# Graph attention on one core: a batch's finishing kept in its PSUM bank, the key matrix placed ahead of a batch's last set, and one unit of work given from GpSimd to ScalarE

## The chip, the cores and the metric

The kernel runs on one core of a Trainium2 chip. The metric is the time of one execution on the device in microseconds (us); several executions were timed and the median is given. The engines are called PE (TensorE, matrix products), DVE (VectorE), ACT (ScalarE), POOL (GpSimd) and SP (SyncE, which issues the DMAs here).

## The reference

The input is x, 8 batches of 1024 rows with 64 channels, and one 1024 x 1024 adjacency matrix per batch. Four graph layers follow one another, each as `x = layernorm(x + layer(x, adj))`. The change concerns the first two, which compute an additive score through a hidden layer of 64 channels for every pair of rows:

```
# layer 0
h   = relu(fa[:, :, None, :] + fb[:, None, :, :])      # fa, fb = feat @ W1 parts
att = softmax(einsum('bijo,o->bij', h, W2) + mask)
out = einsum('bij,bjc->bic', att, feat)
# layer 1
lr     = leaky(vu[:, :, None, :] + iv[:, None, :, :])
scores = where(adj > 0, einsum('bijc,c->bij', lr, yita), -1e12)
agg    = leaky(softmax(scores) @ x)
out    = leaky((agg + (1 + beta) * x) @ linW.T + linb)
```

Layer 2 is a plain graph attention and layer 3 an attention with 8 heads and edge biases. The change doesn't touch them.

## The kernel before, in words

`additive_layers` computes the first two layers. There are 16 "batches" in a row, g = 0 to 15: eight of layer 0 (g < nb, nb = 8) and eight of layer 1. Each has 8 tiles j of 128 query rows, so there are K = 128 tiles k. For a tile the scores of 128 rows against 1024 keys are built in one PSUM tensor, `psS`. The hidden values of 4 rows and 32 channels make a unit, a 128 x 1024 fp32 tensor. PE multiplies units by a selection matrix and adds them up in `psS`. The units of a tile stand in 11 sets (s = 0 to 10) of four, one for each group q of 32 rows.

Units are made in three ways (`unit_sets`):

- A "merged" unit covers 64 channels at once. POOL clamps the keys `BLOS` into a slot of the ring `hid_p` (`clamp_unit`), and DVE takes a maximum of the upper keys, adds POOL's half and writes the slot in place (`merge_units`, one scalar_tensor_tensor). There are 20 in a tile.
- A "pool" unit is a half (32 channels) that POOL makes alone. The tuple POOL_ALONE lists them: 2 in a tile.
- "high" and "low" units are halves that ACT makes as a Relu with a bias (`hidden_units`) into the ring `hid_a`: 22 in a tile.

So POOL makes 22 units in a tile, DVE 20 and ACT 22. Both rings have 11 slots; a slot is free again when PE has used its set (`hid_used`). The upper keys of DVE come from PSUM (`psB`, put there by PE in `place_keys` at the start of a batch), except in sets 0 and 1 of a batch's first tile, where DVE reads a copy in SBUF, `BHI`.

One tile later the softmax of a tile follows: DVE subtracts the mask and takes the minimum (`masked_min`, after its units of set 0), ACT takes the exponential (`exponentials`, set 1), PE transposes (`turn`, set 3), ACT and DVE each copy one half to SBUF (`copy_low`, `copy_high`, set 5), and PE weighs the rows (`weigh`, a tile later).

When the 8 tiles of a batch are through, the batch g - 1 is finished during the tiles of g. The steps stand at fixed places (tile j, set s) in each engine's order, `aux_jobs` for PE and ACT and `batch_steps` for DVE: PE's `fold` writes the bank `psA` in tile 2, DVE's `scale` divides it by the softmax sums at (2, 7) and writes `y` in SBUF, and then `add_rows` (residual, bn_stats, bn_aggr) and `normalise` (subtract the mean, multiply by the deviation) work on `y`. Layer 1 has leaky_relu, a query product and a linear map between them. POOL computes the deviation in `inverse_deviation`, and in tile 3 the bounds of the next batch (`bounds`). In the same tiles the next batch is projected: PE transposes its rows (`turn_x`, also in `psA`) and makes queries, low keys and high keys, one job in tile 0's set 3 and one at the end of each of the tiles 0, 1 and 2. ACT copies each result to SBUF; the last three at its set 0 of the next tile.

The order of every engine is written out by hand; there is no planner.

Of the kernel before, what the change touches and what calls it, by code (L numbers as in the profile page):

```python
# [12 lines left out]
P = 128  # L13
# [10 lines left out]
POOL_ALONE = ((1, 3), (3, 7))  # L24
# [25 lines left out]
def additive_layers(nc, adj, X, rest, later, w, buf, small, ident, nb, n):  # L50
# [64 lines left out]
    with ExitStack() as ctx:  # L115
# [90 lines left out]
        def _(pe):  # L206
            def aux(k, job):
# [7 lines left out]
                if what == "turn_x":  # L215
                    if layer:
                        pe.wait_ge(x_written, g - nb + 1)
                    elif g == 1:
                        pe.wait_ge(rest_loaded, 16)
                    pe.nop(nofuse=True)  # L220
# [98 lines left out]
            for job in projection(0):  # L319
                aux(0, job)  # L320
            for k in range(K + tiles):
                g, j = divmod(k, tiles)
                if k < K and j == 0:
                    place_keys(g)
# [4 lines left out]
                for s in range(SETS):  # L329
                    if k < K:  # L330
                        hidden_set(k, s)
                    if s == 3:
                        if 1 <= k < K + 1:
                            turn(k - 1)
                        for job in aux_jobs(k, 0):
                            aux(k, job)
# [4 lines left out]
        def _(act):  # L341
# [32 lines left out]

            def exponentials(k):
# [21 lines left out]
            for k in range(K + tiles):  # L397
                for s in range(SETS):
# [11 lines left out]
                    if s == 6:  # L410
                        for job in aux_jobs(k, 0):
                            aux(job)

        @block.vector
        def _(dve):
            def merge_units(k, s):
                g, j = divmod(k, tiles)
                if j == 0 and s == 0:
                    dve.wait_ge(aux_out, done("keys_high", g))
                    dve.wait_ge(bounds_ready, 4 * (g + 1))  # L420
                if j == 0 and s == 2:
                    dve.wait_ge(keys_placed, g + 1)
                for i, at_set, q, p in MERGED_UNITS:
                    if at_set == s:
                        at, m = k * NP + i, quad(j, q, p)
                        keys = BHI[:, g % 2, :] if j == 0 and s < 2 else psB[:, :]
                        dve.wait_ge(pool_made, at + 1)
                        dve.scalar_tensor_tensor(out=hid_p[:, at % RING_P, :], in0=keys, scalar=THI[:, g % 2, m:m + 1],  # L428
# [17 lines left out]
            def scale(g):  # L446
# [4 lines left out]
                dve.tensor_tensor(per_tile(y), per_tile(psA[:, :]), spread(rden), ALU.mult).then_inc(aux_out, 1)  # L451

            def add_rows(g):
# [4 lines left out]
                dve.tensor_tensor(y, y, rows(g), ALU.add).then_inc(y_ready, 1)  # L458
                dve.wait_ge(y_ready, g + 1)
                for t in range(tiles):  # L460
                    last = dve.bn_stats(stats[:, t, :], y[:, t * C:(t + 1) * C])
# [7 lines left out]
            def leaky_rows(g):  # L469
                dve.wait_ge(aux_out, done("fold", g))  # L470
                dve.scalar_tensor_tensor(out=y, in0=y, scalar=GAT_SLOPE, in1=y, op0=ALU.mult,
                                         op1=ALU.max).then_inc(leaky, 1)
                dve.wait_ge(leaky, g - nb + 1)
                dve.scalar_tensor_tensor(out=y, in0=rows(g), scalar=w["beta1"], in1=y, op0=ALU.mult,
                                         op1=ALU.add).then_inc(u_ready, 1)

            def linear_out(g):
                dve.wait_ge(aux_made, done("linear", g))
                dve.tensor_tensor(y.rearrange("p (h t c) -> p h t c", h=2, c=C),
# [3 lines left out]
                dve.wait_ge(aux_out, done("linear", g))  # L483
                dve.scalar_tensor_tensor(out=y, in0=y, scalar=GAT_SLOPE, in1=y, op0=ALU.mult,
                                         op1=ALU.max).then_inc(lin_leaky, 1)

            def normalise(g):
                dve.wait_ge(rstd_ready, g + 1)
                dve.tensor_tensor(per_tile(y), per_tile(y), mv[:, :, 0:1].to_broadcast([P, tiles, C]),
# [3 lines left out]
                dve.tensor_tensor(per_tile(out), per_tile(y), spread(rstd), ALU.mult).then_inc(x_written, 1)  # L493

            def batch_steps(g, j, s):
                if (j, s) == (2, 7):
                    scale(g)
                if g < nb:
                    if (j, s) == (2, 9):
                        add_rows(g)  # L500
                    if (j, s) == (4, 8):
                        normalise(g)
                else:
                    if (j, s) == (2, 9):
                        leaky_rows(g)
                    if (j, s) == (4, 2):
                        linear_out(g)
                    if (j, s) == (4, 9):
                        add_rows(g)
                    if (j, s) == (6, 8):  # L510
                        normalise(g)
# [939 lines left out]
```

## Time and profile before

| what | value |
|---|---|
| median of 3 runs | 5577.21 us (5561.33 to 5579.57) |
| the profiled execution's own time | 5561.66 us |
| its span, first to last instruction | 5559.8 us |
| mean granted TensorE clock | 0.942 |
| busy share of the span: PE, DVE, ACT, POOL | 84%, 93%, 84%, 74% |
| stage of the first two layers | 20 us to about 3828 us |

The busy share of an engine is the time in which it had an instruction, over the span. It is an average over stages with different limits. Durations of neighbouring instructions on one engine overlap a little, so what one costs in a row is read from the distance between two starts (called the pitch below).

### The profile page before, as it was taken

The page shows a single profiled execution, that of the slowest core. Times are in us where ns is not written, and L with a number is a line of the kernel's source. Part 1 is how long each engine was busy: PE and PEld are TensorE (multiplying, and loading weights), DVE is VectorE, ACT ScalarE, POOL GpSimd, SP SyncE. Part 2 cuts the span into 40 slices and gives each one's busy share as a digit, 9 for nine tenths or more (in the row PEclk, how much of TensorE's full clock was granted, in tenths as well). Part 3 has the DMA queues.
Part 4 walks back from the last instruction along what each step waited for, and adds up shares of the span by engine and source line. Part 5 has one row for each costly group of instructions (what it writes and reads, how often), then busy time and mean ns, then how long its engine had stood idle before and what let it go on. Part 6 is the DMA issues. An engine that isn't in the chain of part 4 may idle for free. (4 is left out here: it accounts for less than half of the span.)

```text
span 5559.8 us, 118931 instructions
## 1 busy us (share of the span) xinstructions
PE 4678.2 (84%) x48920; PEld 1837.8 (33%) x48920; DVE 5196.5 (93%) x5731; ACT 4667.0 (84%) x5649; POOL 4098.1 (74%) x3706
## 2 busy tenths in 40 slices
PE   7878788787887888888887888887789999999998
PEld 2222222222222222222222222223445554545444
DVE  7999999999999999999999999996769999999998
ACT  7889888898888888888887888886768888888887
POOL 8999999999999999999999999994312322222223
PEclk9999999999999999999999999998879999999999
DMA  1000000000000000000000000003510111011100
GB/s 41 20 20 20 16 20 20 20 20 16 20 20 20 17 20 20 16 20 20 16 20 20 16 20 19 18 16 96 156 34 27 34 34 34 26 34 34 37 26 15
DMA packets 144928, 155.32 MB, mean 28 GB/s; under 512 B 52294, under 2 KB 119622, under 8 KB 144390
## 3 DMA queue, kind: packets, MB, share of 16 engines
q1 hardware_dynamic: 143686, 147.65, 8.9%
q8 instruction: 391, 6.41, 0.5%
q14 instruction: 147, 1.20, 0.1%
q10 hardware_dynamic: 704, 0.07, 0.0%
HBM read 137.20 MB, written 2.10 MB: 25 GB/s over the span
## 5 line engine op out<-in xcount | busy, mean ns | idle before, releaser
L189 POOL TENSOR_SCALAR a_hid_p<-a_BLOS,a_PHI,a_PLO 128x1024 f32<-128x1024 f32 x2816 | 3356.8, 1206 | 164.0 <-PE apsS L315 150.7
L428 DVE SCALAR_TENSOR_TENSOR a_hid_p<-apsB,a_THI,a_hid_p 128x1024 f32<-128x1024 f32 x2496 | 3006.6, 1275 | 40.0 <-POOL a_hid_p L189 39.6
L315 PE MATMUL apsS<-a_hid_p,a_sel_high 128*32 128x512 f32 x11264 | 2680.7, 610 | 151.6 <-DVE a_hid_p L428 58.8
L315 PE MATMUL apsS<-a_hid_a,a_sel_high 128*32 128x512 f32 x6144 | 1927.3, 608 | 187.7 <-DVE a_hid_p L428 179.7
L315 PE MATMUL apsS<-a_hid_a,a_sel_low 128*32 128x512 f32 x5120 | 1718.1, 613 | 289.3 <-DVE a_hid_p L428 266.0
L353 ACT ACTIVATE a_hid_a<-a_BHI,a_ALH 128x1024 f32<-128x1024 f32 x1536 | 1679.7, 1143 | 0.0
L353 ACT ACTIVATE a_hid_a<-a_BLO,a_ALH 128x1024 f32<-128x1024 f32 x1280 | 1423.3, 1143 | 0.0
L315 PEld LDWEIGHTS apsS<-a_hid_p,a_sel_high 128*32 128x32 f32 x11264 | 613.7, 111 | 918.6 <-issue 545.2
L746 PE MATMUL m3S<-xT,Q 64*128 64x512 f32 x2048 | 601.7, 662 | 133.1 <-ACT x_even L790 90.2
L315 PEld LDWEIGHTS apsS<-a_hid_a,a_sel_low 128*32 128x32 f32 x5120 | 371.5, 111 | 864.1 <-DVE a_hid_p L428 578.1
L315 PEld LDWEIGHTS apsS<-a_hid_a,a_sel_high 128*32 128x32 f32 x6144 | 423.8, 110 | 704.4 <-DVE a_hid_p L428 383.2
L762 PE MATMUL m3O<-ZT,Xr 32*64 32x256 f32 x16384 | 576.7, 413 | 4.3 <-DVE ZT L839 4.3
L790 ACT ACTIVATE x_even<-m3S,bias 128x512 f32<-128x512 f32 x684 | 435.1, 690 | 142.0 <-PE m3S L746 120.5
L676 POOL TENSOR_TENSOR part<-prod 128x256 f32<-128x256 f32 x64 | 46.9, 732 | 581.9 <-DVE prod L865 581.9
L839 DVE STREAM_TRANSPOSE ZT<-x_even 128x1024 f32<-128x1024 f32 x342 | 421.8, 1236 | 54.0 <-ACT x_even L799 49.9
L762 PEld LDWEIGHTS m3O<-ZT,Xr 32*64 32x64 f32 x16384 | 358.0, 142 | 319.4 <-issue 222.0
L830 DVE CUSTOM_DVE_ANT_0 x_even<-x_even,mask 128x1024 f32<-128x1024 f32 x342 | 439.8, 1320 | 6.3 <-ACT x_even L790 5.9
L380 ACT ACTIVATE a_Z<-a_Z,small 128x1024 f32<-128x1024 f32 x128 | 146.9, 1148 | 316.4 <-DVE small L437 316.4
L799 ACT ACTIVATE x_even<-x_even,low 128x1024 f32<-128x1024 f32 x342 | 394.7, 1154 | 0.0
L689 POOL TENSOR_SCALAR vare<-mv 128x1 f32<-128x1 f32 x64 | 12.2, 190 | 394.7 <-DVE mv L878 394.7
L746 PEld LDWEIGHTS m3S<-xT,Q 64*128 64x128 f32 x2048 | 162.9, 190 | 335.9 <-ACT x_even L790 175.4
L790 ACT ACTIVATE Z<-m3S,bias 128x512 f32<-128x512 f32 x340 | 216.2, 690 | 61.8 <-PE m3S L746 50.8
(185 smaller groups left out, 4526.5 us busy)
## 6 DMA issues: line engine op xcount, KB each, us to landing
a_adj_in<-adj SPq DMA_DIRECT2D x128, 512.0 KB, 3.4
adj_in<-adj SPq DMA_DIRECT2D x128, 512.0 KB, 3.7
Xr<-x_odd SPq DMA_DIRECT2D x128, 64.0 KB, 2.1
out<-yn SPq DMA_DIRECT2D x64, 32.0 KB, 1.5
x_even<-x SPq DMA_DIRECT2D x1, 256.0 KB, 2.8
wqT<-L_wqT SPq DMA_DIRECT2D x1, 130.0 KB, 4.2
wkT<-L_wkT SPq DMA_DIRECT2D x1, 130.0 KB, 4.3
wvT<-L_wvT SPq DMA_DIRECT2D x1, 130.0 KB, 4.4
```

Source lines behind the costliest of these rows:

```text
L189: gp.tensor_scalar(hid_p[:, at % RING_P, :], BLOS[:, g % 2, :], PHI[:, g % 2, m:m + 1], PLO[:, g % 2, m:m + 1], ALU.min, ALU.max).then_inc ...
L315: last = pe.matmul(psS[32 * q:32 * q + 32, h * HALF:(h + 1) * HALF], sel[:, 28 - 4 * p:60 - 4 * p], unit, start=s == 0 and layer == 0, sto ...
L353: act.activation(hid_a[:, at % RING_A, :], keys[:, g % 2, :], ACT.Relu, bias=ALH[:, g % 2, int(kind == "high"), m:m + 1]).then_inc(act_mad ...
L380: act.activation(Z, Z, ACT.Exp, bias=lowest(k), scale=-1.0, accum_out=den[:, g % 2, j:j + 1]).then_inc(probs_ready, 1)
L428: dve.scalar_tensor_tensor(out=hid_p[:, at % RING_P, :], in0=keys, scalar=THI[:, g % 2, m:m + 1], in1=hid_p[:, at % RING_P, :], op0=ALU.ma ...
L676: gp.tensor_tensor(part[:, 0:4 * C], prod[:, 0:4 * C], prod[:, 4 * C:8 * C], ALU.add).then_inc(halved, 1)
L746: last = pe.matmul(psS[(at + e) % 3][:, :], Q[rows, t % 2, h, :], xT[rows, b % 2, half * HALF:(half + 1) * HALF], start=True, stop=True)
L762: last = pe.matmul(psO[C * e:C * e + C, a, 0:32 * HEADS], Xr[rows, b % 2, at * C:(at + 1) * C], ZT[rows, m % 3, at, :], start=step == 0, s ...
L790: act.activation(Z(k, e)[:, half * HALF:(half + 1) * HALF], psS[(4 * k + 2 * half + e) % 3][:, :], ACT.Prelu, bias=bias[:, b % 2, head:hea ...
L799: act.activation(Z(k, e), Z(k, e), ACT.Exp, bias=low[:, k % 4, e:e + 1], scale=-1.0, accum_out=den[:, m % 8, 2 * h + e:2 * h + e + 1]).the ...
L830: dve.tensor_tensor_reduce(out=Z(k, e), in0=Z(k, e), in1=mask[:, m % 2, :], scale=1.0, scalar=-LOWEST, op0=ALU.add, op1=ALU.min, accum_out ...
L839: dve.transpose(ZT[:, m % 3, :, at:at + 32], Z(k, e).rearrange("p (b i) -> p b i", i=32)).then_inc(turned, 1)
```

## The change

1. DVE no longer writes the batch's rows to `y` in SBUF after each step: `scale`, `add_rows`, `linear_out` and `normalise` read and write the PSUM bank `psA` in place. `y` keeps only the query rows of layer 1.
2. The two leaky_relu steps of layer 1 go from DVE (scalar_tensor_tensor on `y`) to ACT (Prelu in place in `psA`), at (2, 9) and (4, 5).
3. `normalise` moves from (4, 8) in layer 0 and (6, 8) in layer 1 to (7, 10) in both; `add_rows` of layer 1 moves from (4, 9) to (4, 8). The first PE job of a later batch waits for the `normalise` that used `psA` last.
4. PE runs `place_keys` of the next batch ahead of the last set of the current one, where it used to run at the start of the batch. DVE reads `psB` for all its units, and waits for the placed keys at a batch's first unit.
5. The unit (q, s) = (1, 3) leaves POOL_ALONE: a tile now has 21 POOL units, 20 DVE units and 23 ACT units.

```diff
-POOL_ALONE = ((1, 3), (3, 7))
+POOL_ALONE = ((3, 7),)
...
                 if what == "turn_x":
-                    if layer:
-                        pe.wait_ge(x_written, g - nb + 1)
-                    elif g == 1:
+                    if g == 1:
                         pe.wait_ge(rest_loaded, 16)
+                    if g >= 3:
+                        pe.wait_ge(x_written, g - 2)
...
+            place_keys(0)
             for k in range(K + tiles):
                 g, j = divmod(k, tiles)
-                if k < K and j == 0:
-                    place_keys(g)
...
                 for s in range(SETS):
+                    if s == SETS - 1 and j == tiles - 1 and g + 1 < G:
+                        place_keys(g + 1)
...
+            def leaky_rows(g):
+                act.wait_ge(aux_out, done("fold", g))
+                act.activation(psA[:, :], psA[:, :], ACT.Prelu, alpha=GAT_SLOPE).then_inc(leaky, 1)
+
+            def leaky_linear(g):
+                act.wait_ge(aux_out, done("linear", g))
+                act.activation(psA[:, :], psA[:, :], ACT.Prelu, alpha=GAT_SLOPE).then_inc(lin_leaky, 1)
...
+                    if g - 1 >= nb and (j, s) == (2, 9):
+                        leaky_rows(g - 1)
+                    if g - 1 >= nb and (j, s) == (4, 5):
+                        leaky_linear(g - 1)
...
                 if j == 0 and s == 0:
-                    dve.wait_ge(aux_out, done("keys_high", g))
                     dve.wait_ge(bounds_ready, 4 * (g + 1))
-                if j == 0 and s == 2:
                     dve.wait_ge(keys_placed, g + 1)
...
-                        keys = BHI[:, g % 2, :] if j == 0 and s < 2 else psB[:, :]
-                        dve.scalar_tensor_tensor(out=hid_p[:, at % RING_P, :], in0=keys, scalar=THI[:, g % 2, m:m + 1],
+                        dve.scalar_tensor_tensor(out=hid_p[:, at % RING_P, :], in0=psB[:, :], scalar=THI[:, g % 2, m:m + 1],
...
-                dve.tensor_tensor(per_tile(y), per_tile(psA[:, :]), spread(rden), ALU.mult).then_inc(aux_out, 1)
+                dve.tensor_tensor(per_tile(psA[:, :]), per_tile(psA[:, :]), spread(rden), ALU.mult).then_inc(aux_out, 1)
...
-                dve.tensor_tensor(y, y, rows(g), ALU.add).then_inc(y_ready, 1)
+                dve.tensor_tensor(psA[:, :], psA[:, :], rows(g), ALU.add).then_inc(y_ready, 1)
...
-            def leaky_rows(g):
-                dve.wait_ge(aux_out, done("fold", g))
-                dve.scalar_tensor_tensor(out=y, in0=y, scalar=GAT_SLOPE, in1=y, op0=ALU.mult,
-                                         op1=ALU.max).then_inc(leaky, 1)
+            def query_rows(g):
                 dve.wait_ge(leaky, g - nb + 1)
-                dve.scalar_tensor_tensor(out=y, in0=rows(g), scalar=w["beta1"], in1=y, op0=ALU.mult,
+                dve.scalar_tensor_tensor(out=y, in0=rows(g), scalar=w["beta1"], in1=psA[:, :], op0=ALU.mult,
                                          op1=ALU.add).then_inc(u_ready, 1)
...
-                dve.tensor_tensor(per_tile(y), per_tile(y), mv[:, :, 0:1].to_broadcast([P, tiles, C]),
+                dve.tensor_tensor(per_tile(psA[:, :]), per_tile(psA[:, :]), mv[:, :, 0:1].to_broadcast([P, tiles, C]),
                                   ALU.subtract).then_inc(centred, 1)
...
-                dve.tensor_tensor(per_tile(out), per_tile(y), spread(rstd), ALU.mult).then_inc(x_written, 1)
+                dve.tensor_tensor(per_tile(out), per_tile(psA[:, :]), spread(rstd), ALU.mult).then_inc(x_written, 1)
...
                 if g < nb:
                     if (j, s) == (2, 9):
                         add_rows(g)
-                    if (j, s) == (4, 8):
-                        normalise(g)
                 else:
-                    if (j, s) == (2, 9):
-                        leaky_rows(g)
+                    if (j, s) == (3, 1):
+                        query_rows(g)
                     if (j, s) == (4, 2):
                         linear_out(g)
-                    if (j, s) == (4, 9):
+                    if (j, s) == (4, 8):
                         add_rows(g)
-                    if (j, s) == (6, 8):
-                        normalise(g)
+                if (j, s) == (7, 10):
+                    normalise(g)
```

## Rows read from the trace of the kernel before

**Rows 1.** The page: span and busy time of each engine.

```profile
span 5559.8 us, 118931 instructions
...
PE 4678.2 (84%) x48920; PEld 1837.8 (33%) x48920; DVE 5196.5 (93%) x5731; ACT 4667.0 (84%) x5649; POOL 4098.1 (74%) x3706
```

**Rows 2.** Busy time in a stretch, then clock, DMA share, GB/s: first two layers.

```profile
20.00:3802.00 3782.00, 3133.53 (x27208) 979.03 (x27204) 3657.89 (x3285) 3215.44 (x3297) 3592.58 (x3038) 0.95 0.06 19
```

**Rows 3.** The line of `masked_min` (L437): duration ns min/median/max, first and last start.

```profile
L437 DVE CUSTOM_DVE_ANT_0 a_Z<-apsS,a_mask x128: 1206/1217/1226, 59.5 to 3801.1; 128x1024 f32<-128x1024 f32 x128
```

**Rows 4.** The same view: DVE's merged units, `normalise`, `add_rows` and `scale`.

```profile
L428 DVE SCALAR_TENSOR_TENSOR a_hid_p<-apsB,a_THI,a_hid_p x2496: 1248/1276/1287, 34.7 to 3797.6; 128x1024 f32<-128x1024 f32 x192
L428 DVE SCALAR_TENSOR_TENSOR a_hid_p<-a_BHI,a_THI,a_hid_p x64: 1273/2050/5594, 26.0 to 3567.8; 128x1024 f32<-128x1024 f32 x64
...
L489 DVE TENSOR_TENSOR a_y<-a_y,a_mv x16: 693/7959/8877, 391.9 to 3826.2; 128x512 f32<-128x512 f32 x16
...
L458 DVE TENSOR_TENSOR a_y<-a_y,x_even x8: 7049/7066/7076, 331.8 to 1967.2; 128x512 f32<-128x512 f32 x8
...
L451 DVE TENSOR_TENSOR a_y<-apsA,a_rden x16: 691/691/692, 326.4 to 3813.1; 128x512 f32<-128x512 f32 x16
```

**Rows 5.** DVE in order of time: start us, us, line, op, count [idle before].

```profile
1266.76 7.07 DVE L458 TENSOR_TENSOR a_y<-a_y,x_even 128x512 f32<-128x512 f32 x1
...
1275.64 4.82 DVE L428 SCALAR_TENSOR_TENSOR a_hid_p<-apsB,a_THI,a_hid_p 128x1024 f32<-128x1024 f32 x4
...
1345.02 1.23 DVE L437 CUSTOM_DVE_ANT_0 a_Z<-apsS,a_mask 128x1024 f32<-128x1024 f32 x1 [0.80 <-PE apsS L315]
...
1357.50 13.19 DVE L428 SCALAR_TENSOR_TENSOR a_hid_p<-apsB,a_THI,a_hid_p 128x1024 f32<-128x1024 f32 x11
1370.61 1.22 DVE L437 CUSTOM_DVE_ANT_0 a_Z<-apsS,a_mask 128x1024 f32<-128x1024 f32 x1
```

**Rows 6.** POOL in order of time.

```profile
24.66 9.97 POOL L189 TENSOR_SCALAR a_hid_p<-a_BLOS,a_PHI,a_PLO 128x1024 f32<-128x1024 f32 x5
...
1220.42 25.82 POOL L189 TENSOR_SCALAR a_hid_p<-a_BLOS,a_PHI,a_PLO 128x1024 f32<-128x1024 f32 x22
...
1247.47 12.91 POOL L189 TENSOR_SCALAR a_hid_p<-a_BLOS,a_PHI,a_PLO 128x1024 f32<-128x1024 f32 x11
...
1284.27 0.20 POOL L162 TENSOR_SCALAR a_vare<-a_mv 128x8 f32<-128x8 f32 x1
1284.55 1.65 POOL L164 TENSOR_TENSOR a_rstd<-a_vare,small 128x8 f32<-128x8 f32 x1
...
1293.74 0.41 POOL L172 TENSOR_SCALAR a_THI<-a_ALH 128x256 f32<-128x256 f32 x1
...
1296.30 11.73 POOL L189 TENSOR_SCALAR a_hid_p<-a_BLOS,a_PHI,a_PLO 128x1024 f32<-128x1024 f32 x10
```

**Rows 7.** ACT in order of time.

```profile
1226.53 0.58 ACT L393 ACTIVATE a_OT<-apsO 128x512 f32<-128x512 f32 x1
1227.01 1.15 ACT L353 ACTIVATE a_hid_a<-a_BHI,a_ALH 128x1024 f32<-128x1024 f32 x1
1228.05 1.15 ACT L353 ACTIVATE a_hid_a<-a_BLO,a_ALH 128x1024 f32<-128x1024 f32 x1
...
1245.36 1.03 ACT L366 ACTIVATE a_BLO<-apsT 128x1024 f32<-128x1024 f32 x1 [1.09 <-PE apsT L227]
1246.28 2.18 ACT L353 ACTIVATE a_hid_a<-a_BLO,a_ALH 128x1024 f32<-128x1024 f32 x2
```

**Rows 8.** PE in order of time: the low keys' projection.

```profile
1244.18 1.13 PE L227 MATMUL apsT<-a_xT,a_keys_low 64*128 64x512 f32 x4
```

**Rows 9.** Busy time of PE, PEld, DVE, ACT, POOL in single tiles, then the clock.

```profile
1271.10:1308.50 37.40, 27.65 (x224) 8.18 (x226) 34.98 (x44) 25.72 (x27) 34.20 (x32) 0.86 0.05 15
...
1371.70:1397.30 25.60, 22.45 (x200) 6.68 (x200) 25.60 (x24) 24.64 (x25) 25.42 (x23) 1.00 0.04 7
...
3238.00:3263.60 25.60, 23.43 (x211) 7.12 (x209) 25.57 (x23) 24.31 (x26) 25.14 (x22) 1.00 0.02 4
```

More of the change, by code:

```diff
@@ L397, in _ @@
             for k in range(K + tiles):
+                g, j = divmod(k, tiles)
                 for s in range(SETS):
@@ L457, in add_rows @@
                     dve.wait_ge(lin_leaky, g - nb + 1)
-                dve.tensor_tensor(y, y, rows(g), ALU.add).then_inc(y_ready, 1)
+                dve.tensor_tensor(psA[:, :], psA[:, :], rows(g), ALU.add).then_inc(y_ready, 1)
                 dve.wait_ge(y_ready, g + 1)
                 for t in range(tiles):
-                    last = dve.bn_stats(stats[:, t, :], y[:, t * C:(t + 1) * C])
+                    last = dve.bn_stats(stats[:, t, :], psA[:, t * C:(t + 1) * C])
                 last.then_inc(stats_ready, 1)
@@ L478, in linear_out @@
                 dve.wait_ge(aux_made, done("linear", g))
-                dve.tensor_tensor(y.rearrange("p (h t c) -> p h t c", h=2, c=C),
+                dve.tensor_tensor(psA.rearrange("p (h t c) -> p h t c", h=2, c=C),
                                   psT.rearrange("p (h t c) -> p h t c", h=2, c=C)[:, :, 0:4, :],
@@ L482, in linear_out @@
                                   ALU.add).then_inc(aux_out, 1)
-                dve.wait_ge(aux_out, done("linear", g))
-                dve.scalar_tensor_tensor(out=y, in0=y, scalar=GAT_SLOPE, in1=y, op0=ALU.mult,
-                                         op1=ALU.max).then_inc(lin_leaky, 1)
             def normalise(g):
                 dve.wait_ge(rstd_ready, g + 1)
-                dve.tensor_tensor(per_tile(y), per_tile(y), mv[:, :, 0:1].to_broadcast([P, tiles, C]),
+                dve.tensor_tensor(per_tile(psA[:, :]), per_tile(psA[:, :]), mv[:, :, 0:1].to_broadcast([P, tiles, C]),
                                   ALU.subtract).then_inc(centred, 1)
```

## The prediction

> **What bounds the kernel now.** I read the page first: VectorE is busy 93% of the span, no other engine over 84% [rows 1]. That is an average over four layers, so next comes the stretch of the first two layers: VectorE 3657.9 of 3782 us (97%), GpSimd 3592.6 (95%), ScalarE 3215.4 (85%) [rows 2]. The time that I have to account for is the distance between the first and the last masked minimum, 3801.1 - 59.5 = 3741.6 us for 127 tiles, 29.46 us a tile [rows 3].
>
> Then single tiles, where the reader is to see two kinds. In a quiet one the distance between two masked minima is 1370.61 - 1345.02 = 25.59 us and VectorE has no gap [rows 5]. In one with finishing work it is 37.4 us, and there no engine is full: VectorE 34.98, GpSimd 34.20, PE 27.65, ScalarE 25.72 [rows 9]. The view by line says why. `normalise`'s subtraction takes 7959 ns in the median and 693 at its fastest, the residual add 7066, while `scale`, of the same 128x512 size, takes 691 in all its 16 runs [rows 4]. The difference lies in the operands: the long ones read two SBUF tensors, `scale` reads one in PSUM and one in SBUF. The merged unit agrees: with the keys in PSUM 1248 to 1287 ns over 2496 of them, with the keys in SBUF (BHI) up to 5594 [rows 4]. I take the long ones to wait for a pause of GpSimd, which runs its units back to back: the one fast subtraction is within reach of the last one, at 3826.2, when GpSimd has no units left [rows 4]. When the wait is over, GpSimd has filled its ring, PE has run dry, and the granted clock of that tile is 0.86 against 1.00 in the quiet ones [rows 9]. So the stage is bound by VectorE, by its own 25.6 us a tile plus these waits.
>
> **The change, part by part, as load of each engine.** Once the waits are gone, each engine's own work for one batch of 8 tiles decides. I add it up from pitches.
>
> *VectorE.* Quiet tiles: 8 x 25.59 = 204.7 us [rows 5]. `scale`: 0.69 plus about 0.2 for the reciprocal. `add_rows`: from its start to the next unit 1275.64 - 1266.76 = 8.88 us, of which 7.07 is the add [rows 5]; in PSUM I price the add at `scale`'s 0.69 [rows 4], so 2.5. `normalise`: two at 0.69, 1.4. Sum 209.5. Layer 1 has the query rows and the linear output more, 0.69 each: 210.9. The two leaky steps leave. BHI's units cost the same as all others now.
>
> No row shows VectorE writing PSUM in place. The bounds are 0.69 us (a read from PSUM with one from SBUF, `scale`) and 7 to 8 us (the present steps) [rows 4]; I take 0.69, because in all rows the number of SBUF inputs separates short from long, and the new forms have one.
>
> Is PSUM the slower source? `scale` takes 691 ns from PSUM, the subtraction 693 from SBUF when nothing holds it up [rows 4]: no difference, so I charge none. The Trainium skill speaks against the change here: its page "VectorE: DVE Perf Modes" (section "The TRN2 errata") gives 120 fixed cycles with a PSUM source and 58 with an SBUF source. By it each of the six or so steps of a batch would cost 65 ns more, 0.4 us a batch and 6 us in the whole; by the rows, nothing.
>
> *GpSimd.* From one tile's units to the next with the mask between: 1247.47 - 1220.42 = 27.05 us; one unit is 25.82 / 22 = 1.17 [rows 6]. With 21 units 25.88, so 207.0 for 8 tiles. The deviation costs 0.20 + 1.65, the bounds 1296.30 - 1293.74 = 2.56 [rows 6]. Sum 211.4.
>
> *ScalarE.* A quiet tile holds 24.64 us of work [rows 9]; one more unit at the pitch 1228.05 - 1227.01 = 1.04 [rows 7] makes 25.68, or 205.4 for 8. Per batch come four copies of 128x512 (two of OT, the transposed rows, the queries) at 1227.01 - 1226.53 = 0.48 and two of 128x1024 at 1246.28 - 1245.36 = 0.92 [rows 7]: 3.8. Three of the copies wait for PE: the projection runs behind the tile's last set, and ScalarE has only two units in between. After its last unit of set 10 PE needs some 1.75 us for the set (estimated as a tile's 22.45 us of PE [rows 9] over 13 pieces of like size) and 1.13 for the projection [rows 8], ScalarE's two units last 2.1: about 0.9, and the one in the rows waited 1.09 [rows 7]. Three at 1.0 are 3.0. Sum 212.2. Layer 1 adds the copy of the turned rows and the two leaky steps. No row shows Prelu in PSUM: between nothing and 1.04, a unit twice its size; I take the copy's 0.48, same size. Sum 213.6. Waits that the leaky steps add: at (2, 9) ScalarE needs VectorE's `scale` of (2, 7), at (4, 5) its `linear_out` of (4, 2). ScalarE is tied to VectorE at set 1 of every tile (the exponential waits for the minimum), after which both run at 2.1 to 2.4 us a set, so VectorE is there two sets earlier. VectorE waits for them at (3, 1) and (4, 8), three sets later. I cost these at nothing; if that cover were gone, behind the waiting leaky step stand ScalarE's own units, and PE behind them.
>
> *PE.* 22.45 us of a 25.6 us tile, 23.43 in layer 1 [rows 9]. `place_keys` is four products like the projection's, 1.13 [rows 8]. It now starts after a batch's last merge, and the last set stands behind it on PE, whose end the next minimum waits for. VectorE meanwhile runs `normalise` (1.4) and two units (2.4), 3.8 us, while PE needs 1.1 + 1.75 = 2.9. So neither VectorE nor the minimum waits; only the first batch has no `normalise` to cover it, about 1 us once. The moved `normalise` and the new wait of `turn_x` cost nothing: the normalise it waits for ends three sets, some 7 us, before. No DMA moves; they are 6% busy [rows 2].
>
> **The sum.** A batch can't be shorter than its fullest engine: 212.2 us in layer 0, 213.6 in layer 1. If nothing of the engines' extra work lay beside each other's, it would be GpSimd's 207.0 and all extras: 4.4 + 4.8 + 6.8 = 223.0, and 225.8 in layer 1. The rings of 11 units hold 11 x 1.17 = 12.9 us of GpSimd, more than any engine's extras of a whole batch, so most is absorbed; but four engines within 2% of one another always lose something at the joints. I go one sixth of the way: 214.0 and 215.6.
>
> Start: GpSimd's first five units took 9.97 us where their pitch is 5.9, because VectorE's BHI units alternated with them [rows 6]. That saves 4.1, the missing unit 1.2: the first minimum comes at 59.5 - 5.3 = 54.2. Batch 0 has no finishing: 207.0 + 2.6 = 209.6. Then 8 x 214.0 (finishing of layer 0) + 6 x 215.6, and 186 for the last seven tiles (215.6 less a tile, less the missing projection). Last minimum: 54.2 + 209.6 + 1712.0 + 1293.6 + 186 = 3455.4, against 3801.1: 345.7 us less. The tail behind it has an idle GpSimd and gains nothing; layers 2 and 3 stay. The profiled execution's 5561.7 (span 5559.8) becomes 5216. The median shown is 15.5 us above it, and its lowest run equals it; I add 6 and predict 5222.
>
> By the fullest engine alone the last minimum comes at 3427, for a time of 5188; with nothing overlapped at 3599, for 5359.
>
> **Rivals.**
>
> *The joints eat more (B).* ScalarE, idle for 15% of the stage so far [rows 2], becomes the fullest engine, and it has the waits in its order: the exponential for VectorE, three copies and the leaky steps for PE and VectorE. Each lateness of one engine then adds to the next. For: all four engines are at 88 to 100% of a tile. Against: the rings. It gives 5260 to 5359, say 5310.
>
> *PSUM in place doesn't free VectorE (C).* If the add and the subtraction still waited, because one operand is still SBUF or because the output matters, a batch would be 209.5 + (7.07 - 0.69) + (7.96 - 0.69) = 223.1 and 224.5 in layer 1. Last minimum about 54 + 210 + 1785 + 1347 + 195 = 3591: 5352. Against it: `scale` and 2496 merged units with just these inputs [rows 4]. The Trainium skill, "SBUF — State Buffer", section "Who interferes with whom", says that a VectorE instruction with at most one SBUF input, outside the 2-port modes, doesn't contend with GpSimd; by that rule C doesn't happen.
>
> *Slower (D): PE becomes the bound through its clock.* PE needs 22.45 us of a tile at a granted clock of 1.00 [rows 9]. If the denser stage were granted less, PE would be the bound from 22.45 / 29.46 = 0.76 on, in layer 1 from 0.80; below it the kernel is slower than before. At 0.70 tiles would be 32.1 and 33.5 us, the stage 64 x 32.1 + 64 x 33.5 = 4198, some 430 us longer: 5990. Against it: the clock fell to 0.86 just where PE had been kept waiting, and was 1.00 where it was densest [rows 9]; 1.00 is the level of 2.4 GHz, 0.86 a mean of that and 1.2 GHz.
>
> **How the numbers follow.** The forecast (5175 to 5255): 0.68. B: 0.21. C: 0.05. D: 0.03. Nothing gained, as D near its threshold or a wait that I haven't seen: 0.02. Below 5175: 0.01. The range 5175 to 5320 holds the forecast and most of B, a bit over 0.8. A difference of 0.3% is about what a measurement of this kernel can tell from none. Faster by more: 0.95; within: 0.02; slower: 0.03.
>
> **What would show it.** Right: the residual add and both steps of `normalise` at about 0.69 us; no merged unit over 1.3; quiet tiles of 25.7 to 26.2 us in place of 25.6 to 27.0, and no tile over 31; ScalarE at 97% or more of the stage, and its waits for the minimum, now the largest, mostly gone; the granted clock of the stage near 1.00; first minimum near 54, last near 3455. Wrong: steps in `psA` at several us (C), tiles over 28 with ScalarE waiting at the exponential or the leaky steps (B), a clock under 0.9 without PE waiting (D).

## The result and the profile after

| | median, us | range of the runs |
|---|---|---|
| before | 5574.09 | 5561.33 to 5579.57 |
| changed | 5247.68 | 5239.73 to 5251.13 |

The ratio is 0.9415, 95% interval 0.9395 to 0.9436: about 326 us less. The forecast was 5222 in a range of 5175 to 5320. The page of the changed kernel, as in [rows 1]:

```profile
span 5237.9 us, 118915 instructions
...
PE 4645.1 (89%) x48920; PEld 1850.3 (35%) x48920; DVE 4898.1 (94%) x5715; ACT 4792.2 (91%) x5793; POOL 3857.7 (74%) x3578
```

The stage of the first two layers, against [rows 2], then three single tiles, against [rows 9]: one with `scale` and `add_rows`, a quiet one, and one of layer 1. The columns are busy time of PE, PEld, DVE, ACT and POOL, then clock, DMA share and GB/s:

```profile
20.00:3480.00 3460.00, 3096.98 (x27200) 987.81 (x27202) 3359.09 (x3271) 3342.91 (x3439) 3354.39 (x2910) 1.00 0.07 21
```

```profile
1158.73:1189.26 30.53, 24.95 (x222) 9.24 (x222) 28.85 (x42) 26.56 (x27) 26.36 (x24) 1.00 0.07 23
1216.70:1242.30 25.60, 23.01 (x204) 7.05 (x204) 25.52 (x23) 25.60 (x27) 25.42 (x23) 1.00 0.06 21
2861.90:2890.00 28.10, 25.16 (x240) 7.89 (x224) 26.18 (x25) 26.60 (x28) 27.03 (x25) 1.00 0.10 36
```

VectorE, ScalarE and GpSimd are now busy for 97% of the stage each. The tile with `scale` and `add_rows` takes 30.5 us where it took 37.4, the quiet one is what it was, and the clock is 1.00 (2.4 GHz) in all three. The first window of [rows 9] doesn't run from one masked minimum to the next; the tile from minimum to minimum, with the same columns, is this one, as long and as loaded:

```profile
1244.45:1281.89 37.44, 26.47 (x222) 9.37 (x222) 35.27 (x42) 25.55 (x26) 34.78 (x31) 0.86 0.10 29
```

By line (duration ns min/median/max, first and last start), against [rows 3, 4]:

```profile
L448 DVE CUSTOM_DVE_ANT_0 a_Z<-apsS,a_mask x128: 1211/1222/1228, 55.4 to 3479.9; 128x1024 f32<-128x1024 f32 x128
...
L439 DVE SCALAR_TENSOR_TENSOR a_hid_p<-apsB,a_THI,a_hid_p x2560: 1250/1278/1296, 27.1 to 3476.4; 128x1024 f32<-128x1024 f32 x197
...
L494 DVE TENSOR_TENSOR apsA<-apsA,a_mv x16: 695/701/707, 453.6 to 3504.7; 128x512 f32<-128x512 f32 x16
...
L469 DVE TENSOR_TENSOR apsA<-apsA,x_even x8: 687/690/693, 318.4 to 1829.9; 128x512 f32<-128x512 f32 x8
...
L462 DVE TENSOR_TENSOR apsA<-apsA,a_rden x16: 699/700/700, 313.1 to 3491.8; 128x512 f32<-128x512 f32 x16
```

```profile
L378 ACT ACTIVATE apsA<-apsA x8: 572/580/584, 2045.3 to 3492.5; 128x512 f32<-128x512 f32 x8
...
L382 ACT ACTIVATE apsA<-apsA x8: 574/590/599, 2091.1 to 3499.4; 128x512 f32<-128x512 f32 x8
```

The subtraction fell from 7959 ns to 701, the residual add from 7066 to 690, no merged unit is over 1.3 us, and a leaky step in PSUM takes what a copy does. The last masked minimum starts at 3479.9 where it started at 3801.1: 321.2 us earlier.

### The profile page after: what moved, and what is told of

Read it like the earlier page. It is cut to its first block and busy times, and to the rows that moved or that the text cites. A ratio compares the mean times of both kernels' runs of the same rounds, so it can differ in the third digit from the quotient of the medians.

```text
span 5237.9 us, 118915 instructions
## 1 busy us (share of the span) xinstructions
PE 4645.1 (89%) x48920; PEld 1850.3 (35%) x48920; DVE 4898.1 (94%) x5715; ACT 4792.2 (91%) x5793; POOL 3857.7 (74%) x3578
## 5 line engine op out<-in xcount | busy, mean ns | idle before, releaser
L189 POOL TENSOR_SCALAR a_hid_p<-a_BLOS,a_PHI,a_PLO 128x1024 f32<-128x1024 f32 x2688 | 3151.9, 1193 | 79.7 <-PE apsS L315 67.1
L439 DVE SCALAR_TENSOR_TENSOR a_hid_p<-apsB,a_THI,a_hid_p 128x1024 f32<-128x1024 f32 x2560 | 3078.4, 1279 | 15.9 <-POOL a_hid_p L189 14.0
L315 PE MATMUL apsS<-a_hid_p,a_sel_high 128*32 128x512 f32 x10752 | 2644.9, 599 | 191.6 <-ACT a_hid_a L354 117.4
L315 PE MATMUL apsS<-a_hid_a,a_sel_low 128*32 128x512 f32 x5632 | 1682.5, 597 | 95.5 <-DVE a_hid_p L439 52.7
L354 ACT ACTIVATE a_hid_a<-a_BLO,a_ALH 128x1024 f32<-128x1024 f32 x1408 | 1569.5, 1144 | 0.0
L315 PEld LDWEIGHTS apsS<-a_hid_p,a_sel_high 128*32 128x32 f32 x10752 | 584.6, 109 | 964.1 <-issue 548.1
L692 POOL TENSOR_SCALAR vare<-mv 128x1 f32<-128x1 f32 x64 | 12.2, 190 | 394.3 <-DVE mv L881 394.3
L793 ACT ACTIVATE Z<-m3S,bias 128x512 f32<-128x512 f32 x340 | 215.5, 688 | 60.8 <-PE m3S L749 49.4
L842 DVE STREAM_TRANSPOSE ZT<-Z 128x1024 f32<-128x1024 f32 x170 | 210.2, 1237 | 26.8 <-ACT Z L802 24.7
```

Of the source, the lines that this page charges most:

```text
L189: gp.tensor_scalar(hid_p[:, at % RING_P, :], BLOS[:, g % 2, :], PHI[:, g % 2, m:m + 1], PLO[:, g % 2, m:m + 1], ALU.min, ALU.max).then_inc ...
L315: last = pe.matmul(psS[32 * q:32 * q + 32, h * HALF:(h + 1) * HALF], sel[:, 28 - 4 * p:60 - 4 * p], unit, start=s == 0 and layer == 0, sto ...
L354: act.activation(hid_a[:, at % RING_A, :], keys[:, g % 2, :], ACT.Relu, bias=ALH[:, g % 2, int(kind == "high"), m:m + 1]).then_inc(act_mad ...
L439: dve.scalar_tensor_tensor(out=hid_p[:, at % RING_P, :], in0=psB[:, :], scalar=THI[:, g % 2, m:m + 1], in1=hid_p[:, at % RING_P, :], op0=A ...
L793: act.activation(Z(k, e)[:, half * HALF:(half + 1) * HALF], psS[(4 * k + 2 * half + e) % 3][:, :], ACT.Prelu, bias=bias[:, b % 2, head:hea ...
L842: dve.transpose(ZT[:, m % 3, :, at:at + 32], Z(k, e).rearrange("p (b i) -> p b i", i=32)).then_inc(turned, 1)
```

## The experiments

What lies behind the last masked minimum (layers 2 and 3) took from 1758.0 to 1770.2 us in the profiled runs of kernels that have the same code there. For parts of a few us I therefore read the start of the last masked minimum, from the same row as above, beside the ratio. Each ratio is to the kernel before as it ran beside that kernel, with medians from 5560 to 5574 us, so the medians in the tables differ by up to 0.3% from what the ratios give:

| kernel | ratio to before (95%) | median | last minimum | against the changed kernel |
|---|---|---|---|---|
| changed | 0.9415 (0.9395 to 0.9436) | 5248 | 3479.9 | |
| y in SBUF | 0.9556 (0.9543 to 0.9569) | 5323 | 3557.0 | +77.1 |
| BHI in two sets | 0.9474 (0.9461 to 0.9487) | 5276 | 3507.5 | +27.6 |
| keys placed late | 0.9472 (0.9459 to 0.9485) | 5274 | 3510.8 | +30.9 |
| unit back on GpSimd | 0.9563 (0.9550 to 0.9576) | 5327 | 3565.0 | +85.1 |
| normalise early | 0.9486 (0.9473 to 0.9498) | 5275 | 3505.2 | +25.3 |
| y in SBUF and unit back | 0.9727 (0.9714 to 0.9740) | 5415 | 3653.9 | +174.0 |
| no leaky steps | 0.9427 (0.9414 to 0.9439) | 5250 | 3482.2 | +2.3 |
| copies behind set 1 | 0.9324 (0.9312 to 0.9337) | 5183 | 3423.4 | -56.5 |

| the kernel before, with | ratio to before (95%) | median | last minimum | against before (3801.1) |
|---|---|---|---|---|
| the unit moved alone | 0.9703 (0.9689 to 0.9716) | 5398 | 3625.7 | -175.4 |
| GpSimd made to pause | 0.9823 (0.9809 to 0.9836) | 5463 | 3702.8 | -98.3 |
| the mask behind unit 0 | 0.9756 (0.9740 to 0.9772) | 5433 | 3670.4 | -130.7 |
| copies behind set 1 | 0.9982 (0.9973 to 0.9991) | 5558 | 3797.7 | -3.4 |

### The finishing back in SBUF

```diff
-                dve.tensor_tensor(psA[:, :], psA[:, :], rows(g), ALU.add).then_inc(y_ready, 1)
+                dve.tensor_tensor(y, y, rows(g), ALU.add).then_inc(y_ready, 1)
```

and the same for the other steps, ScalarE's leaky ones too.

> The changed kernel with one thing undone: scale, add_rows, linear_out, normalise and the two leaky steps work on y in SBUF, at the same places and on the same engines as in the changed kernel. My theory (a VectorE step with two SBUF inputs waits for a pause of GpSimd): the residual add at 4 to 7 us and the subtraction of normalise at 5 to 9 us in place of 0.70, 10 to 14 us a batch, so 150 to 220 us longer than the changed kernel's 5248: 5400 to 5470. Rival (the steps were long because of where they stood, next to steps since moved to ScalarE and to another set): they stay near 0.7 us and the time stays within 20 us of 5248.

The time is 75 us longer, half of the least that my theory said, and far from the rival. The add and the subtraction:

```profile
L469 DVE TENSOR_TENSOR a_y<-a_y,x_even x8: 1481/1510/1519, 318.2 to 1848.8; 128x512 f32<-128x512 f32 x8
L469 DVE TENSOR_TENSOR a_y<-a_y,x_odd x8: 692/6508/6524, 2119.7 to 3576.5; 128x512 f32<-128x512 f32 x8
```

```profile
L494 DVE TENSOR_TENSOR a_y<-a_y,a_mv x16: 677/943/1382, 455.7 to 3581.2; 128x512 f32<-128x512 f32 x16
```

They wait again, but only the add of layer 1 for long (5.8 us); the add of layer 0 waits 0.8 us and the subtraction 0.25, not 7. Where the operands lie is necessary for the long wait and doesn't set its length. One of the short adds, and GpSimd around it:

```profile
536.76 1.52 DVE L469 TENSOR_TENSOR a_y<-a_y,x_even 128x512 f32<-128x512 f32 x1
```

```profile
530.66 9.85 POOL L189 TENSOR_SCALAR a_hid_p<-a_BLOS,a_PHI,a_PLO 128x1024 f32<-128x1024 f32 x8 [3.43 <-PE apsS L315]
540.60 1.04 POOL L157 TENSOR_SCALAR a_mask<-a_adj_in 128x1024 f32<-128x1024 int32 x1
```

GpSimd had been idle for 3.43 us, waiting for PE to free a slot. The add begins in the sixth unit behind that gap and ends at 538.28, 0.60 us behind the start of the seventh (537.68), in the middle of the row.

### The unit alone, on the kernel before

```diff
-POOL_ALONE = ((1, 3), (3, 7))
+POOL_ALONE = ((3, 7),)
```

> The kernel before with only the unit (1, 3) moved from GpSimd to ScalarE. My theory (the long tiles are bound by VectorE's waits, the quiet ones in part by GpSimd): quiet tiles that took 26.6 to 27.0 go to 25.6 to 25.9, the tiles of 34 to 37 us stay; 3 to 5 us a batch, 50 to 80 us shorter than 5574: 5495 to 5525. Rival (GpSimd's load was the bound all the time and the finishing only a detail): most of the 326 us of the whole change comes from this, under 5400. Second rival (ScalarE can't take a unit): no change or slower.

The first rival was right in size: 165 to 175 us, over half of the whole change, from one unit, where I had said 50 to 80. Its reason, GpSimd's load alone, isn't shown: this run doesn't separate GpSimd's shorter tile from shorter waits. The steps in SBUF got shorter although nothing about them was changed (7066 and 7959 ns in [rows 4]), and the add again begins in the sixth unit behind a gap of GpSimd, here of 2.2 to 2.4 us:

```profile
L458 DVE TENSOR_TENSOR a_y<-a_y,x_even x8: 1510/1520/1527, 325.2 to 1901.2; 128x512 f32<-128x512 f32 x8
...
L489 DVE TENSOR_TENSOR a_y<-a_y,a_mv x16: 692/3299/6702, 380.9 to 3649.0; 128x512 f32<-128x512 f32 x16
```

### GpSimd made to pause

```diff
+    FIRST_OF_LAST_SET = min(i for i, u in enumerate(POOL_UNITS) if u[0] == SETS - 1)
...
                 for i in range(NP):
+                    if g >= 1 and i == FIRST_OF_LAST_SET:
+                        if j == 2:
+                            gp.wait_ge(*((y_ready, g) if g - 1 < nb else (u_ready, g - nb)))
+                        elif j == 4:
+                            gp.wait_ge(*((x_written, g) if g - 1 < nb else (y_ready, g)))
+                        elif j == 6 and g - 1 >= nb:
+                            gp.wait_ge(x_written, g)
                     clamp_unit(k, i)
```

> The kernel before, with GpSimd made to pause: in the tiles with finishing steps (2, 4 and, in layer 1, 6) it waits ahead of its first unit of set 10 until VectorE has ended the SBUF steps that stand there (add_rows' add or the query rows, and normalise). Nothing of VectorE's work changes. My theory (VectorE waits for a pause of GpSimd's stream): the add and the subtraction take 0.7 to 2 us in place of 7 to 8, GpSimd loses its lead but no more than 3 us each time, batches come to 224 to 228 us in place of 233 to 240, and the kernel is 100 to 180 us shorter than 5574. Rival (two SBUF inputs are slow by themselves, or the wait is for the ring or PE): the steps stay at 7 us and GpSimd's wait comes on top, 5574 or more.

Both operands are still in SBUF, and the steps are short. GpSimd's loss of its lead costs VectorE new waits for units, 155.4 us in the stage against 52.7 before, so batches take 228.6 and 232.1 us where I had said 224 to 228, and the gain, 98 us, is just under the 100 to 180 expected:

```profile
L467 DVE TENSOR_TENSOR a_y<-a_y,x_even x8: 680/681/684, 332.8 to 1933.1; 128x512 f32<-128x512 f32 x8
```

```profile
L498 DVE TENSOR_TENSOR a_y<-a_y,a_mv x16: 692/1631/1637, 391.3 to 3727.2; 128x512 f32<-128x512 f32 x16
```

The subtraction begins 0.1 us into a unit, the last ahead of the pause, and waits for that unit alone. So two SBUF inputs aren't slow by themselves: VectorE waits for a break in GpSimd's stream.

### What a break is: the mask behind unit 0

In order of time, VectorE and then GpSimd of the kernel before:

```profile
1326.95 8.68 DVE L489 TENSOR_TENSOR a_y<-a_y,a_mv 128x512 f32<-128x512 f32 x1
```

```profile
1325.69 9.39 POOL L189 TENSOR_SCALAR a_hid_p<-a_BLOS,a_PHI,a_PLO 128x1024 f32<-128x1024 f32 x8
1335.17 1.36 POOL L157 TENSOR_SCALAR a_mask<-a_adj_in 128x1024 f32<-128x1024 int32 x1
```

The subtraction begins just after the second of these eight units, seven pass, and it ends at 1335.63, 0.46 us behind the mask's start; the mask is stretched to 1.36 us from 1.05, its median. The mask seems to be the break. The edit moves it on GpSimd:

```diff
-                    if i == 4:
+                    if i == 0:
                         make_mask(k)
```

> The kernel before with one thing moved: GpSimd computes a tile's mask behind its unit 0 in place of unit 4. In the trace of the kernel before, VectorE's two-input steps end 0.5 us behind the start of the next mask on GpSimd (a subtraction from 1326.95 to 1335.63, the mask at 1335.17), after six or seven units in one row. Theory: GpSimd's row of units has no break but the mask (and a full ring), and VectorE waits for it; with the mask four units earlier the residual add of layer 0 takes 7.07 - 4.7 = 2.4 us and the subtraction 8 - 4.7 = 3.3 us in place of 7.1 and 8 to 9; 60 to 140 us shorter than 5568. Rival (the wait ends when the ring is full or PE has run dry, wherever the mask stands): the steps stay at 7 to 8 us and the time within 20 us of 5568.

The add takes 2314 ns where 2.4 us was expected and 7066 stood before. Again the step ends 0.45 us behind the mask's start (559.86 + 2.31 = 562.17 against 561.72):

```profile
559.86 2.31 DVE L458 TENSOR_TENSOR a_y<-a_y,x_even 128x512 f32<-128x512 f32 x1
```

```profile
561.72 1.37 POOL L157 TENSOR_SCALAR a_mask<-a_adj_in 128x1024 f32<-128x1024 int32 x1
```

The subtraction takes 4.8 us in the median, not 3.3: in layer 0 it now begins four units ahead of the mask, where seven less the four of the move would be three. The kernel is 131 to 136 us shorter, with no work moved off any engine.

The mask isn't the only place where a step gets in. I put together every VectorE step with two SBUF inputs that began during a unit of GpSimd, from the seven traces that have such finishing steps (before, the four other kernels made from it, and the two with `y` in SBUF); without the 15 that a made pause ended, there are 264. Of these, 161 ended 0.45 to 0.46 us behind the start of the next mask, whatever the number of units up to it (at most eight). The other 103 ended 0.56 to 0.64 us behind the start of the very next unit, as the add above did and as `leaky_linear` of the kernel before does. None got in at a unit further on. All 161 had begun in the 15th unit of an unbroken row or later; of the 103, 95 began in one of the first ten units behind a gap or the mask, and 8 further on. So a step soon after a break of GpSimd got in quickly, and one far from it nearly always waited for the next mask. What in the engines makes the difference, and what of the 8, is not shown.

### Both undone together

The edits of the two experiments "finishing back in SBUF" and "unit back on GpSimd" in one kernel.

> Two parts of the change undone together: y in SBUF (alone 75 us) and the unit (1, 3) back on GpSimd (alone 79 us); leaky steps on ScalarE, places and keys as in the changed kernel. The moved unit alone gave the kernel before more than half of the gain, and in it the SBUF steps took 1.5 to 3.6 us in place of 7. Theory formed from that: GpSimd with 22 units is the engine that lags (27.05 us a tile against VectorE's 25.6), so it never waits and gives VectorE no pause; with 21 units it runs ahead, its ring fills, it pauses by itself, and the two-input steps get in. Then the two parts together cost clearly more than the sum: the add and the subtraction at 5 to 8 us again, batches near 232, 5470 to 5510. Rival (the two act apart from each other): 75 + 79 on 5248, 5400, with the steps at 1.5 to 5.6 us as with y in SBUF alone.

```profile
L494 DVE TENSOR_TENSOR a_y<-a_y,a_mv x16: 676/4594/5086, 470.7 to 3678.2; 128x512 f32<-128x512 f32 x16
```

```profile
L469 DVE TENSOR_TENSOR a_y<-a_y,x_even x8: 1612/4156/7095, 325.4 to 1905.8; 128x512 f32<-128x512 f32 x8
L469 DVE TENSOR_TENSOR a_y<-a_y,x_odd x8: 693/9846/9848, 2186.2 to 3673.5; 128x512 f32<-128x512 f32 x8
```

Split verdict. The steps got longer as the theory said, from 1.5 and 0.9 us to 4.2 and 4.6, and from 6.5 to 9.8 in layer 1, though the first two stay under its 5 to 8. The time went nearly as the rival said: +174.0 us, the sum of the parts being 77.1 + 85.1 = 162.2. The theory, as I read it now, had forgotten that with 22 units GpSimd's own work is 220.8 us a batch, and a VectorE that waits up to there costs nothing; the batches came to 223.9 to 229.5 us.

### The unit back on GpSimd

```diff
-POOL_ALONE = ((3, 7),)
+POOL_ALONE = ((1, 3), (3, 7))
```

> The changed kernel with the unit (1, 3) given back to GpSimd: 22 units on GpSimd and 22 on ScalarE. My theory (GpSimd, VectorE and ScalarE are all near the length of a batch): GpSimd's own work is then 8 x 27.05 + 4.4 = 220.8 us a batch against 215.5 to 217 measured, so batches of 221 to 223 and 80 to 110 us longer: 5330 to 5360; no tile under 27.0 in the quiet ones. Rival (ScalarE, with its waits for PE and VectorE, sets the pace): one unit less on it makes the kernel shorter or leaves it within 20 us of 5248.

As my theory had it: batches of 221.1 to 221.5 us, against 220.8 added up, quiet tiles mostly of 27.1, 79 to 85 us longer (the low end). Each batch still has one or two tiles of 25.6 to 25.8 us, behind longer ones that gave GpSimd a lead, so "no tile under 27.0" was wrong. GpSimd's sum is right, and with 22 units on GpSimd it isn't ScalarE that decides.

### The keys: BHI, late placing, an early normalise

```diff
+                if j == 0 and s == 2:
                     dve.wait_ge(keys_placed, g + 1)
...
+                        keys = BHI[:, g % 2, :] if j == 0 and s < 2 else psB[:, :]
```

> The changed kernel with VectorE reading the SBUF copy of the high keys (BHI) in sets 0 and 1 of a batch's first tile, as before; the keys are still placed ahead. My theory: these four units of a batch are two-SBUF-input instructions and alternate with or wait for GpSimd, 1.9 us on average as before in place of 1.28, up to 5 us for the first; 2.5 to 4 us a batch and 4 us at the start, so 40 to 65 us longer than 5248. Rival (the first tile of a batch is bound by something else, GpSimd's or ScalarE's own order): under 10 us.

27.6 us by the last minimum, 29 by the medians, below what I said: 3 of it is the start (first minimum 58.2 against 55.4); the 64 units took 1.62 us on average, not 1.9.

```diff
-            place_keys(0)
...
+                if k < K and j == 0:
+                    place_keys(g)
...
-                    if s == SETS - 1 and j == tiles - 1 and g + 1 < G:
-                        place_keys(g + 1)
```

> The changed kernel with place_keys back at the start of a batch, behind the last set of the one before, VectorE still taking all keys from PSUM. My theory: VectorE's first unit of a batch then waits for the last set (1.75 us) and the products (1.1), of which normalise covers 1.4: a wait of about 1.5 us a batch, 24 us in all, 5272. Rival (the order is worth nothing since PE catches up anyway): within 5 us of 5248.

30.9 us, 24 foretold. The wait is there, 1.8 us a batch where I had said 1.5 (the columns are us in total, times, longest):

```profile
DVE a_hid_p L438 <- PE apsB L287: 21.9, 12, 1.9
...
DVE a_hid_p L438 <- issue: 3.2, 1, 3.2
```

```diff
+                    if (j, s) == (4, 9):
+                        normalise(g)
...
-                if (j, s) == (7, 10):
-                    normalise(g)
+                    if (j, s) == (6, 8):
+                        normalise(g)
```

The first place is in layer 0, the second in layer 1.

> The changed kernel with normalise back at (4, 9) in layer 0 and (6, 8) in layer 1, still in PSUM. My theory: the work is the same, but VectorE reaches the next batch's first unit 1.4 us earlier, when the keys aren't placed yet, and waits about 1.2 us there: 10 to 20 us longer than 5248. Rival (placing is quick enough or the wait is absorbed): within 5 us. Second rival (the place at (7, 10) itself cost something, since the minimum of tile 7 stands behind it): shorter.

25.3 us by the last minimum, where 10 to 20 were foretold. VectorE waits 1.37 us at the first unit of 15 batches (the profile names no releaser; the place is the one where the keys are awaited):

```profile
DVE a_hid_p L439 <- issue: 20.5, 15, 1.4
```

`normalise` at (7, 10) is thus cover for placing the keys, as the prediction costed it.

### The leaky steps left out

Both Prelu instructions are replaced by empty ones that only give the signal; the output lacks the two leaky_relu of layer 1.

> The changed kernel without the two leaky_relu steps of layer 1 on ScalarE (they are left out; only their signals are given, so the output is another). Theory (they cost ScalarE 0.5 us each and nothing else, and cause no wait): 8 batches of layer 1 shorter by at most 1 us, 0 to 8 us in all. Rival (their waits for VectorE delay the chain; batches of layer 1 are 1.5 us longer than those of layer 0): 10 to 20 us shorter, batches of layer 1 at 215.5 as in layer 0.

+2.3 us by the last minimum, a ratio within the interval of the changed kernel. They cost nothing that shows, and the rival is out. Batches took 216.1 to 217.2 us in layer 1 (216.6 on average, 216.9 with the steps) and 215.5 to 217.1 in layer 0 (216.5 on average, 215.9 with the steps, though nothing of layer 0 was touched). So a difference of 1 us between the layers' batches is near what moves from one profiled run to the next, and its cause isn't known.

### The joint: copies behind set 1

ScalarE of the changed kernel in order of time at the start of a tile, and VectorE a little later:

```profile
1156.36 2.18 ACT L354 ACTIVATE a_hid_a<-a_BHI,a_ALH 128x1024 f32<-128x1024 f32 x2
1159.64 1.03 ACT L367 ACTIVATE a_BLO<-apsT 128x1024 f32<-128x1024 f32 x1 [1.10 <-PE apsT L227]
...
1162.64 1.14 ACT L389 ACTIVATE a_Z<-a_Z,small 128x1024 f32<-128x1024 f32 x1
```

```profile
1172.20 0.69 DVE L455 COPY a_PT<-apsT 128x512 f32<-128x512 f32 x1 [1.51 <-PE apsT L264]
```

The copy of the projection waits 1.10 us and takes 0.92; the exponential behind it is late by both, so PE turns the tile late, and VectorE waits 1.51 us at `copy_high`. Such waits of VectorE add up to 57.9 us in the stage, 3.9 in each of the 15 batches that have a projection beside them. The high keys, a tile later, are waited for longer:

```profile
1190.05 1.02 ACT L369 ACTIVATE a_BHI<-apsT 128x1024 f32<-128x1024 f32 x1 [3.85 <-PE apsT L227]
```

The edit:

```diff
-                    if k >= 1 and s == 0:
+                    if k >= 1 and s == 1:
                         for job in aux_jobs(k - 1, 1):
                             aux(job)
```

> The changed kernel with ScalarE's copies of the three projection results moved behind its units of set 1 (ahead of the exponential), where they stood behind set 0. In the changed kernel ScalarE waits 1.2, 1.1 and 3.9 us for PE there, its set 1 and the exponential come late by that, PE turns the tile late, and VectorE waits 1.0 to 1.5 us at copy_high. My theory (these joints are what the forecast's sum had too small): 2 to 4 us a batch, 30 to 60 us shorter than 5248. Rival (VectorE's and GpSimd's own work is the whole batch, ScalarE's lateness only uses up slack): within 10 us.

56.5 us by the last minimum, 51 by the ratios: the best kernel of the study, 5183 us. Its waits at `copy_high`, and one batch of it:

```profile
DVE a_PT L455 <- PE apsT L264: 4.2, 14, 0.3
```

```profile
265.80:478.40 212.60, 190.47 (x1692) 60.02 (x1684) 209.77 (x206) 208.26 (x215) 210.91 (x183) 0.99 0.07 21
```

The waits at `copy_high` fell from 57.9 to 4.2 us, nearly the whole gain. VectorE is busy 209.8 us of the batch, against 209.5 added up in the prediction, GpSimd 210.9 against 211.4, and the batch takes 212.6. The same edit on the kernel before:

> The kernel before with only ScalarE's projection copies moved behind its units of set 1, the move that made the changed kernel 65 us shorter. Theory (the joint counts only where ScalarE is full; before, it was idle for 15% of the stage and waited for VectorE's minimum in the same tiles): within 10 us of 5568. Rival (the move is worth the same everywhere, since VectorE waits at copy_high for the late turn): 40 us shorter or more.

10 us by the ratio, 3.4 by the last minimum, as the theory had it. But its reason isn't shown clean. Before, VectorE waited only 12.2 us at `copy_high`; those waits went, and others came. The subtraction now waits for the mask longer, 9847 ns in the median for 7959:

```profile
L489 DVE TENSOR_TENSOR a_y<-a_y,a_mv x16: 692/9847/9852, 391.1 to 3822.8; 128x512 f32<-128x512 f32 x16
```

The add of layer 1 got shorter (874 ns for 4360), and the waits for units went from 52.7 to 65.0 us. So there was little to gain at this joint before, and the places where steps met the masks shifted as well.

## Why the prediction was right

**What bounds it.** Right in what waits for what: the steps with two SBUF inputs waited for GpSimd, shown by the pauses and by the mask's move. The sentence that VectorE waits "for a pause of GpSimd" until its ring is full and PE has run dry was too coarse. The long waits end at the next mask, which is no pause and needs no full ring, so their length is the distance to the mask; a step that begins soon after a break gets in at the next unit; and whatever moves GpSimd against VectorE changes which of the two it is. That is one reason why parts of the change don't add up: the unit alone gives 175.4 us, all the rest alone 3801.1 - 3565.0 = 236.1, both 321.2 and not 411.5. The other is that a batch can't be shorter than its fullest engine, with 22 units GpSimd at 220.8 us. My single numbers for parts failed there, "y in SBUF" by half and "the unit alone" by more than half. The prediction of the whole didn't depend on them, since it started from the engines' own work with all such waits gone.

**VectorE's steps at 0.69.** 0.69 to 0.70 measured. Writing PSUM in place costs what writing SBUF does, so rival C is out: 700 ns for `scale` with PSUM out against 691 with SBUF out. Reading from PSUM costs little more than reading from SBUF: the add takes 690 ns from PSUM and SBUF against 681 from SBUF alone with GpSimd pausing, the subtraction 701 against 676 to 693 at its fastest. That is 8 to 25 ns, and not the 65 ns that the prediction worked out from the Trainium skill, "VectorE: DVE Perf Modes" (section "The TRN2 errata").

**GpSimd at 211.4, quiet tiles at 25.88, ScalarE's leaky steps at 0.48 each.** Batches of 221.1 to 221.5 with 22 units confirm the first, the rows of ScalarE (580 and 590 ns with overlap) and the run without the leaky steps the last.

**The keys.** First unit not waiting, no cost beyond the first batch: right. In the changed kernel VectorE waited once, 1.4 us.

**The joints, the term that was too small.** I took batches of 214.0 and 215.6 us; they came to 215.9 and 216.9 on average ((1994.4 - 267.5) / 8 and (3295.7 - 1994.4) / 6, from the starts of the minima). With batch 0 at 212.1 for 209.6, the first minimum at 55.4 for 54.2 and the last seven tiles at 184.2 for 186 this is the 24.5 us between 3455.4 and 3479.9. The "one sixth of the way" rested on no row; the batches went about a third of the way in layer 0 and a quarter in layer 1. The error lies in the step that put the three waits for PE, "three at 1.0", into ScalarE's sum alone, and it has two parts. They stand ahead of the exponential, so they pass on through PE to VectorE, the engine that has nothing to spare. And they are longer: 1.15, 1.10 and 3.9 us in most batches of layer 0, some 6 us and not 3. With the copies moved, batches come to 211 to 214. Rival B had named this mechanism. The measured time lies 60 us above the 5188 of the fullest engine alone, where B's 5260 to 5359 lie 72 to 171 above it: inside the forecast's 5175 to 5255, but nearer to B's low end (12 us) than to the 5222 (26 us). That it fell on the forecast's side is a matter of a few us at the joints, which no row had settled. Two of the signs named beforehand weren't met in full: quiet tiles took 25.6 to 27.7 us, not 25.7 to 26.2, and the longest tile 31.1; some tiles of layer 1 are over 28, which was a sign of B.

**Clock.** 1.00 in the stage against 0.95 [rows 2], 1.00 against 0.86 in the tile with `add_rows`, where PE used to be kept waiting; D is out.

## What to carry to other kernels

When an instruction of one engine waits for another engine's stream, ask not only which instructions collide but where that stream has its next break: a short instruction elsewhere in its order was worth 131 us here, and one unit less on it 175 us, over half of the 321 us of the whole change. Add up each engine's own work per period before pricing a change in waits; here VectorE's and GpSimd's sums were right to 0.5 us of 210, and the rest was joints. Once the engines are within 2% of each other, look for copies that wait for a neighbour ahead of an instruction on which a third engine depends, and put work that doesn't wait ahead of them; here that was worth 57 us, in a single try.

## What the runs showed of the hardware

- A VectorE instruction with two SBUF inputs (fp32, 128x512) takes 0.68 to 0.69 us when GpSimd pauses. Against GpSimd's row of tensor_scalar units (1.17 us apart) it either got in at the start of the very next unit (103 of 264 steps, 95 of them begun in one of the first ten units behind a gap or the mask) or waited through up to eight units and ended 0.46 us behind the start of the next instruction of another kind, the mask (161 steps, all begun in the 15th unit of a row or later), both in the kernel before and with the mask moved. I didn't try what makes the mask a break, its semaphore waits and empty instruction, the short gap of 0.08 us ahead of it, or its int32 input.
- With one input from PSUM and one from SBUF, output to SBUF or PSUM, 691 and 700 ns, with GpSimd running.
- An in-place Prelu of 128x512 fp32 in PSUM takes ScalarE 0.58 to 0.59 us, and its copy of that size from PSUM to SBUF 0.58.
